# Second and third attention: weight, vector and row loads moved from the sync engine's queue to GpSimd's

## What is computed

```
# _L0_xattn_ref(hidden_states, encoder_hidden_states, ...):
h = _mha(hidden_states, hidden_states, hidden_states, sa_wq, sa_bq, sa_wk, sa_bk, sa_wv, sa_bv)
x = _ln(hidden_states + h, ln1_g, ln1_b)
h = _mha(x, encoder_hidden_states, encoder_hidden_states, ca_wq, ca_bq, ca_wk, ca_bk, ca_wv, ca_bv)
x = _ln(x + h, ln2_g, ln2_b)
h = jax.nn.relu(x @ fc1_w + fc1_b) @ fc2_w + fc2_b
return _ln(x + h, ln3_g, ln3_b)
# reference:
x = _layernorm(x + _L0_attn_ref(x, L0_attn_wq, ...), axis=-1)
x = _layernorm(x + _L0_xattn_ref(x, ctx_1024, ...), axis=-1)
x = _layernorm(x + _L0_ffn_ref(x, L0_ffn_w1, ...), axis=-1)
```

## Time and profile before

| | |
|---|---|
| time, median of 3 runs | 3251.22 us (3243.08 to 3252.54) |
| profiled execution, time | 3245.53 us |
| its span | 3243.7 us, mean granted TensorE clock 0.978 |
| PE busy | 92% of the span |
| DVE, ACT, POOL busy | 79%, 62%, 42% |
| DMA | 405.86 MB: q1 (SP) 348.64 MB, q0 (GpSimd) 51.40 MB |
| chain that ended last | PE 51%, DVE 18%, DMA 13%, ACT 8%, issue 4%, SP's issues 4%, POOL 1% |

### The profile page before, as it was taken

How to read it: one execution, slowest core, us unless ns; L and a number is a source line. 1 busy time by engine, 2 the same in 40 slices (tenths; PEclk the granted TensorE clock), 3 DMA queues, 4 the chain that set the end, 5 groups by cost and what they waited for, 6 DMA issues and landing times.

```text
span 3243.7 us, 87025 instructions
## 1 busy us (share of the span) xinstructions
PE 2988.8 (92%) x34642; PEld 2369.2 (73%) x34642; DVE 2567.3 (79%) x4750; ACT 1995.7 (62%) x4650; POOL 1349.9 (42%) x1273
## 2 busy tenths in 40 slices
PE   7998999988999769999999999999889999999996
PEld 4987888888899647777877778877765565565662
DVE  4776888888899669999999999999846666666666
ACT  2655565667787537777777777877655445344352
POOL 0675632257765544444344344443132232222232
PEclk9999999999999889999999999999899999999997
DMA  4666655456554546655655555554341121211212
GB/s 127 185 206 223 194 180 153 135 159 202 174 162 140 150 118 134 141 141 125 140 137 134 137 135 147 134 129 106 125 152 40 46 53 53 56 45 44 56 40 49
DMA packets 430834, 405.86 MB, mean 125 GB/s; under 512 B 272368, under 2 KB 346240, under 8 KB 429280
## 3 DMA queue, kind: packets, MB, share of 16 engines
q1 hardware_dynamic: 415600, 348.64, 41.0%
q0 software_dynamic: 14576, 51.40, 5.1%
q10 hardware_dynamic: 256, 0.26, 0.0%
HBM read 239.98 MB, written 109.52 MB: 108 GB/s over the span
## 4 chain that ended last, share of the span: by engine, by line
PE 51%; DVE 18%; DMA 13%; ACT 8%; issue 4%; SPq 4%; POOL 1%; ACTq 0%; DVEq 0%; POOLq 0%
PE at_ps L769 22%; PE at_ps L1430 4%; PE at_ps L911 4%; PE at_ps L855 4%; DVE at_mx_cross L988 4%; DVE at_p L997 3%; DMA self_spill<-at_proj 3%; PE at_ps L1444 3%; PE at_ps L890 3%; PE at_ps L1455 3%; PE at_ps L1411 2%; ACT at_ps L945 2%; DVE at_proj L981 2%; DMA at_o_raw<-at_values 2%; PE at_ps L865 2%
## 5 line engine op out<-in xcount | busy, mean ns | idle before, releaser
L944 ACT ACTIVATE at_p<-at_ps 125x448 f16<-125x448 f32 (+2 forms) x1280 | 676.9, 529 | 285.9 <-PE at_ps L890 196.5
L997 DVE TENSOR_TENSOR at_p<-at_ps,at_p 125x448 f16<-125x448 f32 (+2 forms) x1280 | 750.5, 596 | 129.3 <-ACT at_ps L945 119.3
L945 ACT ACTIVATE at_ps<-at_ps 125x448 f32<-125x448 f32 (+2 forms) x1280 | 679.5, 531 | 0.0
L988 DVE TENSOR_REDUCE at_mx_cross<-at_ps 128x1 f32<-128x750 f32 x512 | 476.7, 931 | 26.9 <-PE at_ps L855 24.5
L1070 POOL TENSOR_TENSOR at_o_sum<-at_o_raw 128x256 f32<-128x256 f32 x192 | 121.2, 631 | 782.6 <-ACT at_o_raw L951 782.1
L911 PE MATMUL at_ps<-at_values,at_p 112*128 112x65 f16 (+3 forms) x6656 | 303.3, 185 | 23.4 <-DVE at_p L997 10.5
L1478 ACT ACTIVATE at_masks<-at_ps,at_b_cols 128x256 f32<-128x256 f32 x224 | 106.7, 476 | 336.2 <-PE at_ps L1411 336.1
L992 DVE TENSOR_REDUCE at_mx<-at_ps 112x2 f32<-112x448 f32 (+1 forms) x512 | 303.9, 609 | 10.0 <-PE at_ps L865 7.0
L1411 PE MATMUL at_ps<-at_xt,at_early 128*128 128x256 f16 x1792 | 302.1, 276 | 8.9 <-ACT at_w_first L1479 6.1
L911 PEld LDWEIGHTS at_ps<-at_values,at_p 112*128 112x128 f16 (+1 forms) x6656 | 267.2, 97 | 49.3 <-ACT at_o_raw L951 19.7
L1430 PE MATMUL at_ps<-at_w_second,at_w_first 128*128 128x512 f16 x896 | 283.6, 379 | 0.0
(11 more groups left out here) (217 smaller groups left out, 6941.7 us busy)
## 6 DMA issues: line engine op xcount, KB each, us to landing
at_x_res<-x SPq DMA_DIRECT2D x124, 256.0 KB, 3.2
cross_spill<-at_proj SPq DMA_DIRECT2D x64, 487.0 KB, 3.2
at_x_rows<-x SPq DMA_DIRECT2D x92, 256.0 KB, 3.1
at_prep<-bit POOLq DMA_DIRECT2D x32, 512.0 KB, 5.5
at_early<-ctx SPq DMA_DIRECT2D x32, 512.0 KB, 5.3
at_stacks<-cross_spill SPq DMA_DIRECT2D x64, 243.5 KB, 3.7
causal_spill<-at_proj SPq DMA_DIRECT2D x64, 224.0 KB, 3.5
at_stacks<-causal_spill SPq DMA_DIRECT2D x128, 112.0 KB, 2.3
```

What stands on the lines that cost most here:

```text
L944: act.activation(mem.p_hi[0:self.KC, n % 4, 0:self.P_COLS], scores, ACT.Exp, scale=EXP_SCALE)
L945: act.activation(scores, scores, ACT.Exp, scale=EXP_SCALE).then_inc(self.exp_done, 1)
L988: dve.tensor_reduce(self.mx[:, at, t, h:h + 1], mem.ps_qk[:, :, 0:self.KT // 2], AX.XY, ALU.max).then_inc(self.max_done, 1)
L997: dve.tensor_tensor(mem.p_lo[0:self.KC, n % 4, cols], mem.ps_st[0:self.KC, self.st_bank(b, g, n), cols], mem.p_hi[0:self.KC, n % 4, cols], ...
```

## The change

These DMAs are issued by GpSimd and no longer by SP, each at the place in GpSimd's list where the event stands in `events`, with the waits that they had: the second and third weights (with `stored_through`, and for the third the wait on `proj_free`), `v_bias`, gain and shift of the self and of the cross attention, the cross attention's x rows (2 for each batch, on new semaphores `cross_rows_in`) and its context rows (4 for each batch). The transposes, spills, stacks, rows of maxima, residuals and stores stay on SP. The number of DMAs and their bytes stay the same; 105 rows leave SP's list (1774 to 1669) and come into GpSimd's (1275 to 1380). The lists of PE, DVE and ACT are unchanged.

```diff
     def sync(self, sp, kind, b, g, n):
         mem, before = self.mem, self.before
-        if kind == "load":
+        if kind == "load" and not self.cross:
...
-        elif kind == "load c":
...
-        elif kind == "weights in":
-
-            for n in range(2):
-                sp.dma_start(self.w_part[n], self.w[n].rearrange("p (c n) -> p c n", c=DC)).then_inc(self.w_in, 16)
-        elif kind == "v bias in":
...
-        elif kind == "norm in":
...
     def gpsimd(self, pool, kind, b, g, n):
         mem, at = self.mem, b - self.b0
-        if kind == "split x":
-            pool.wait_ge(self.x_rows_in[b % 2], 32 * (b // 2 + 1))
+        if kind == "load" and self.cross:
+            pool.wait_ge(self.stored, 32 * (b - self.NB + 1))
+            if self.back(b, 2).cross:
+                pool.wait_ge(self.x_split, b - 1 - self.b0)
+            else:
+                pool.wait_ge(self.proj_full, self.before.full_index["x1", b - 2, 0] + 1)
+            for t in range(2):
+                pool.dma_start(mem.x_rows[0:T // 2, b % 2, t, :], self.x_in[b - self.b0, t * T // 2:(t + 1) * T // 2, :]
+                               ).then_inc(self.cross_rows_in[b % 2], 16)
+        elif kind == "load c":
+            if b == self.b0:
+                pool.wait_ge(self.rows_clear, 1)
+            wait(pool, self.c_split, 3 * (b - self.b0 - 1) + n + 1 if b > self.b0 else 0)
+            rows = self.kv_in[b - self.b0]
+            if n < 2:
+                two = rows[2 * n * P:(2 * n + 2) * P, :].rearrange("(c p) d -> p c d", p=P)
+                pool.dma_start(mem.c_rows[:, 2 * n:2 * n + 2, :], two).then_inc(self.c_rows_in[n], 16)
...
+        elif kind == "weights in":
+
+            for n in range(2):
+                pool.dma_start(self.w_part[n], self.w[n].rearrange("p (c n) -> p c n", c=DC)).then_inc(self.w_in, 16)
+        elif kind == "v bias in":
+            if self.before.norm is not None:
+                pool.wait_ge(self.res_done, self.before.NB)
+            pool.dma_start(mem.v_bias[:, :], self.biases[:, 2 * D:3 * D].partition_broadcast(P)).then_inc(self.v_bias_in, 16)
+        elif kind == "norm in":
...
+        elif kind == "split x":
+            pool.wait_ge(self.cross_rows_in[b % 2], 32 * (at // 2 + 1))
...
-                elif kind == "third weights":
-                    preparation.stored_through(sp, 11)
-                    sp.wait_ge(causal.proj_free, causal.free_index["y1", NB - 1, 0] + 1)
-                    cross.sync(sp, "weights in", cross.b0, 0, 0)
...
+                elif kind == "third weights":
+                    preparation.stored_through(pool, 11)
+                    pool.wait_ge(causal.proj_free, causal.free_index["y1", NB - 1, 0] + 1)
+                    cross.gpsimd(pool, "weights in", cross.b0, 0, 0)
```

More of the change, by code:

```diff
@@ L231, in worked, with stored_through @@
         return self.done, self.number(k, ("split", "round")) + 1
-    def stored_through(self, sp, k):
+    def stored_through(self, pool, k):
         for place in range(2):
             last = max(j for j in range(k + 1) if j % 2 == place)
-            sp.wait_ge(self.stored[place], self.stores[place][last // 2] + 32)
+            pool.wait_ge(self.stored[place], self.stores[place][last // 2] + 32)
     def load(self, pool, m):
@@ L425, in __init__ @@
         self.x_rows_in = [sem("x_rows_in0"), sem("x_rows_in1")]
+        self.cross_rows_in = [sem("cross_rows_in0"), sem("cross_rows_in1")]
         self.x_res_in = [sem("x_res_in0"), sem("x_res_in1")]
@@ L496, in __init__ @@
         self.yg_done, self.y_done, self.v_bias_in, self.gain_in = s.yg_done, s.y_done, s.v_bias_in, s.gain_in
+        self.cross_rows_in = s.cross_rows_in
         self.c_rows_in, self.slots_set, self.rows_clear = s.c_rows_in, s.slots_set, s.rows_clear
@@ L662, in sync @@
         mem, before = self.mem, self.before
-        if kind == "load":
+        if kind == "load" and not self.cross:
             if before is not None:
                 sp.wait_ge(self.stored, 32 * (b - self.NB + 1))
-            if b >= 2 and self.back(b, 2).cross:
-                sp.wait_ge(self.x_split, b - 1 - self.b0)
-            elif b >= 2:
+            if b >= 2:
                 sp.wait_ge(self.proj_full, self.full_index["x1", b - 2, 0] + 1)
             for t, q0 in enumerate(TILES):
-                rows, q0 = (T // 2, t * T // 2) if self.cross else (P, q0)
-                sp.dma_start(mem.x_rows[0:rows, b % 2, t, :], self.x_in[b - self.b0, q0:q0 + rows, :]
+                sp.dma_start(mem.x_rows[:, b % 2, t, :], self.x_in[b - self.b0, q0:q0 + P, :]
                              ).then_inc(self.x_rows_in[b % 2], 16)
-        elif kind == "load c":
[L675 to L685, removed]
         elif self.cross and kind in ("x0", "x1"):
@@ L1042, in gpsimd @@
         mem, at = self.mem, b - self.b0
-        if kind == "split x":
-            pool.wait_ge(self.x_rows_in[b % 2], 32 * (b // 2 + 1))
+        if kind == "load" and self.cross:
[15 more added lines that the diff above has]
+                pool.dma_start(mem.c_rows[:, 2 * n:2 * n + 2, :], two).then_inc(self.c_rows_in[n], 16)
+            else:
+                for c in (4, 5):
+                    n_rows = min(P, self.KT - c * P)
+                    pool.dma_start(mem.c_rows[0:n_rows, c, :], rows[c * P:c * P + n_rows, :]).then_inc(self.c_rows_in[n], 16)
+        elif kind == "weights in":
[6 more added lines that the diff above has]
+        elif kind == "norm in":
+            if self.before.norm is not None:
+                pool.wait_ge(self.y_done, self.before.NB)
+            pool.dma_start(mem.gain[:, :], self.norm[0].partition_broadcast(P)).then_inc(self.gain_in, 16)
+            pool.dma_start(mem.shift[:, :], self.norm[1].partition_broadcast(P)).then_inc(self.gain_in, 16)
+        elif kind == "split x":
+            pool.wait_ge(self.cross_rows_in[b % 2], 32 * (at // 2 + 1))
             if at >= 1:
```

13 lines of the change are left out of this document (3 added, 10 removed).

## The result

The changed kernel takes 3256.48 us (median of 22 runs, 3236.18 to 3273.27), the kernel before 3244.97 us in its 22 runs (3239.78 to 3258.49). The ratio is 1.0033, interval 1.0021 to 1.0044: slower by 7 to 14 us, where 13.6 us less were forecast. The profiled execution of the changed kernel took 3250.01 us with a span of 3247.6. It lies 6.5 us under its median, so it shows a mild case; a second trace of the same kernel has a span of 3258.1 us and is used beside it.

A forecast was written before the change was run, and what follows sets the result against it. PE, busy for 92% of the span, was taken as the bound, so gains come only from its idle stretches; terms -8.6 - 2 + 0 - 2 - 1 = -13.6 gave 3237.6 us from the median 3251.22, range 3224 to 3252.

The forecast's parts named there:

- A: Second weights: moving five DMAs off SP ends PE's 9.4 us stop; -8.6 us, from -11.6 to -3.6.
- the 3 us put back: Second weights: PE's stop expected to remain, because spill and stack land at about twice their undisturbed time beside the weights.
- The 2.2 us of slow clock: Second weights: twelve matmuls behind the old stop took 4.94 us instead of 2.75; this loss was to vanish.
- B: Third weights: PE's waits of 5.1 us go, 3 come back; -2 us, from -5 to +5.
- rival 2: Weights hold the DMA engines about as before, so sharing keeps PE's stop; -4.6 us, 3246.6; chance 0.21.
- rival 3: Stacks formerly ahead of second and third weights are caught beside them; +12 us, 3263; chance 0.06.
- The rule of the Trainium skill: DMAs from different engines interleave on the same 16 DMA engines; spreading saves only issue time, -2.9 at the second weights.
- C: Crossing: SP's relief and GpSimd's 3.8 us delay of at_z cancel; 0 us, from -6 to +4.
- D: Second cross batch: earlier spill removes half of PE's 4.3 us wait; -2 us, from -4.3 to +0.8.
- E: Steady cross stage, 14.5 batches: SP has next to nothing to give; -1 us, from -4 to +2.
- Rival 1: Crossing is relieved too, its chain being SP's and not GpSimd's; some 9 us more gained, 3229; chance 0.15.
- Rival 4: Crossing: GpSimd's issues each wait out a VectorE operation, 7 us more ahead of at_z; 3244.6; chance 0.03.

The follow-up runs named there:

- e13: Kernel before, all loads on SP, with 14 small GpSimd operations, 10 us in all, added ahead of at_z at the crossing; ratio 1.0019, 6 us slower.

## Why the prediction was wrong

**A, second weights: mechanism right, size off.** Forecast -8.6, measured -3.8 by the fit and -3.5 by the stage table. The stop for the row of maxima went as told. The term that failed is the 3 us put back: PE's stops for stacks there sum to 4.2 to 11.1 us in the eight traces with this burst, 6.8 in the mean (0.7 in the six with the burst on SP). The working took a stack beside the weights at twice its time, 4.6 us, and the trace made again shows 14: "at twice that, the stack of 293.95 lands near 300" is the sentence. The 2.2 us of slow clock that were to go along with the old stop also came back in part: 3.7 us at a granted clock of 0.54 behind the first new stop in the changed trace, about 1.7 us lost (an estimate from these two numbers).

**B, third weights: wrong sign.** Forecast -2, range to +5; measured +6.9 (fit), +5.8 (table). The step that failed is the same doubling, "at twice 2.3 us it lands at 729.5". It landed after 9.5 to 11.7 us. PE's stops for stacks from 705 to 760 us sum to 10.9 us in the mean of the six traces with these weights on GpSimd, to 6.0 in the six with them on SP: 4.9 us more, where 5.1 were to go. Behind it stands how I read the earlier trace rows: nearly packet for packet, hence nobody held up. Packet for packet was right. But in that window SP's queue held weights, 1.80 MB in 338 packets, 5.3 KB each; stacks and spills go in packets of 0.8 KB, and the same turn by turn gave them 7.9% of the engines in place of 63.6%. The text named this as what would make it wrong, as the ground of rival 2, at 0.21, and as rival 3, at 0.06. Rival 3 had its place and its threshold right (a stack that takes over 9 us in place of 2.3). It expected +5 or more at each of the two loads; at the second weights a removed stop of 9.4 covered it, at the third nothing did. The rule of the Trainium skill that was weighed ("DMA: Bandwidth & Descriptors", "Issuing engines are not separate DMA queues") had A at -2.9, nearer to the measured value than mine. That only issue time is saved isn't what the traces show, though: the 9.4 us stop went and other stops came, and the two nearly cancel. The pieces don't settle it: their 16 issues take 7.2 us on SP, and the kernels with them on SP and on GpSimd differ by 9 us with intervals of 4 to 6 us either way.

**C, crossing: the link right, its size and its worth wrong.** VectorE's wait was forecast at 3 to 4 us and was 5.4 to 6.9 in all eight traces (up to 3.4 in the nine with the rows on SP); the stage cost 3.6 us where 0 was told and +4 was the end of the range. "VectorE is then late by as much as SP is early" failed: SP's relief (the spill of 1084.89 in the changed trace had its stack issued 2.0 us later, the one of 1081.24 before took 6.85) is worth nothing while VectorE, and PE behind it, wait for GpSimd. The late kernel, e13, shows that GpSimd's lateness alone costs this much; no kernel moves GpSimd's loads to a place behind `at_z`, so it isn't shown that this is all of the 3.6 us. A smaller slip: the relief was put at seven issues and 3.4 us, and the chain of before has six of them, 2.5 us.

**D, second cross batch.** Forecast -2, measured +0.3. The spill went out early, but I hadn't seen that GpSimd's loads, freed of SP's order, all become issuable at the same moment, beside SP's transposes, and stretch them from 8.1 to 13.5 us and more.

**E, steady.** Forecast -1, measured +0.9 with a scatter of as much: as told, nothing.

**Rows, the remainder.** The fit has 6.2 us for the rows; the stages have 3.6 + 0.3 + 0.9, and 2.0 behind 2306 us, where no load is moved. Why the last should be slower after rows on GpSimd isn't known, and with 8 and 7 traces it may be scatter. Nor is it shown in which batches the rows cost: less the fitted -3.8 and +6.9, the kernel with only the first three batches' rows leaves +2.7 us for them, the one with only the later ones +5.0, each with some 6 us either way.

**Rivals.** Rival 1 (the crossing relieved) didn't come about. Rival 2 had A right, both its size, -3.6, and its reason, small packets that each wait for a large one; it missed the time because it put the third weights at 0 and the rest at -1. Rival 3's total, +12, is near the measured +10.7, but in part by luck: it had A at +5.6 in place of -3.8, which is made up for in part by the third weights (+6.9 for its +5) and the rows (+6.2 for its +2). Rival 4, issues stretched by VectorE, didn't come about: GpSimd's issues took 0.5 to 0.8 us each in the rows above. The median that the forecast started from, 3251.22 of three runs, lay 6 us above that of 22 runs, 3244.97; the terms are compared here and not the total, which this shifts. The bar of 0.3% under which no difference was to be told was set too high: the intervals are 0.11 to 0.25% either way.

## What to carry to other kernels

A second DMA queue protects small, urgent transfers from big ones only by turns: count packets and their size on both sides, and expect a transfer of many packets under 1 KB to take as many big packets of the other queue as it has of its own. When loads move to another engine's list, ask which urgent transfers stood ahead of them and now don't; one wait for those gave 6 and 11 us here against the same kernel without it, the loads in pieces 11 to 13 us. And an engine at 42% can be the bound at one place: look for the instruction that is waited for within a microsecond of its end, since what is put ahead of it can count nearly in full (8.5 of 9.2 us here).

## What the runs showed of the hardware

Beside a queue of 11 KB packets, a queue of 0.8 KB packets moved as many (215 against 223 in 7 us) and had 7.9% of the DMA engines, and a 112 KB transfer that otherwise takes 2.2 us took 9.5. Six DMA transposes that fill SP's queue for 8.1 us (ten traces, 8.1 to 8.2) take 13.5 to 19.1 us when 1.9 to 2.4 MB of loads are issued on GpSimd's queue in the same microseconds (eight traces); the time shows as the duration of SP's issues. The issue of a DMA of 1.5 MB on GpSimd took 0.54 to 0.57 us, with VectorE busy for 2.1 of the 2.8 us around the first two, no longer than that of one of 256 KB (0.54).
